# The first context and Wk requested on ScalarE's queue instead of SyncE's, in a gated cross-attention layer

## What is computed

```python
def attention(x, y, Wq, bq, Wk, bk, Wv, bv, Wo, bo):
    q, k, v = split_heads(x @ Wq + bq), split_heads(y @ Wk + bk), split_heads(y @ Wv + bv)
    weights = softmax(q @ k.T / sqrt(32))
    return merge_heads(weights @ v) @ Wo + bo

def quantised_layer(x, weight_q, weight_scale, bias):
    x_scale = maximum(max(abs(x), axis=-1), 1e-6) / 127
    x_q = int8(clip(round(x / x_scale), -128, 127))
    return (x_q @ weight_q.T) * x_scale * weight_scale + bias

x = x + tanh(g_xattn) * attention(layernorm(x), ctx, ...)
x = x + tanh(g_ffn) * quantised_layer(layernorm(x), ...)
```

## Time and profile before

| what | us |
|---|---|
| median of 3 runs | 813.43 (812.89 to 814.37) |
| the profiled execution, its own time | 812.92 |
| its span in the profile | 811.0 |
| TensorE busy | 791.6 |
| VectorE busy | 575.5 |
| ScalarE busy | 555.6 |
| GpSimd busy | 517.4 |

### The profile page before, as it was taken

One profiled execution on the slowest core, in us unless ns is written; L12 is line 12 of the kernel. 1 busy time (PEld: TensorE's weight loads), 2 busy tenths in 40 slices (PEclk: granted clock), 3 DMA queues, 4 the chain that ended last, 5 costly groups with the idle time before them and its releaser, 6 DMA issues.

```text
span 811.0 us, 17119 instructions
## 1 busy us (share of the span) xinstructions
PE 791.6 (98%) x6629; PEld 521.2 (64%) x6658; DVE 575.5 (71%) x916; ACT 555.6 (69%) x845; POOL 517.4 (64%) x518
## 2 busy tenths in 40 slices
PE   8899999999999999999999999999999999999995
PEld 6665667666666666666666666667667666666563
DVE  4878677686767767677586757867678575767668
ACT  5676587676776767676676775767677666777685
POOL 4626484765758566594765758567494765756587
PEclk9999999999999999999999999999999999999998
DMA  8531605142241422315232151422314131111112
GB/s 292 217 83 75 201 28 163 60 144 71 66 132 53 162 79 59 112 53 167 74 117 74 48 172 53 144 79 66 123 54 143 66 92 54 40 53 53 53 52 104
DMA packets 39631, 79.68 MB, mean 98 GB/s; under 512 B 6912, under 2 KB 8320, under 8 KB 37504
## 3 DMA queue, kind: packets, MB, share of 16 engines
q1 hardware_dynamic: 38976, 77.75, 29.8%
q10 hardware_dynamic: 576, 0.85, 0.3%
HBM read 61.78 MB, written 16.81 MB: 97 GB/s over the span
## 4 chain that ended last, share of the span: by engine, by line
PE 89%; DVE 3%; issue 3%; POOL 2%; ACT 1%; DMA 1%; SPq 0%; DVEq 0%; ACTq 0%; POOLq 0%
PE bank_a L340 25%; PE bank_b L340 24%; PE scores L395 8%; PE sum_ps L424 7%; PE scores L412 7%; PE pv_ps L428 6%; PE bank_a L472 3%; PE scores L415 2%; PE pv_ps L472 2%; PE bank_b L472 1%; DVE row_max L1092 1%; PE bank_b L447 1%; PE sum_ps L403 1%; PE bank_a L447 1%; DMA wk_stage<-in_wk 1%
## 5 line engine op out<-in xcount | busy, mean ns | idle before, releaser
L1092 DVE TENSOR_REDUCE row_max<-scores 128x16 f32<-128x1920 f32 x64 | 138.1, 2158 | 109.0 <-PE scores L395 109.0
L773 ACT ACTIVATE probs<-scores 120x2048 f32<-120x2048 f32 x64 | 120.4, 1882 | 77.3 <-PE scores L415 77.2
L1445 POOL TENSOR_TENSOR x<-x,u_sb 128x512 f32<-128x512 f32 x56 | 75.8, 1353 | 127.3 <-DVE u_sb L1181 125.0
L1440 POOL TENSOR_TENSOR x<-x,gbias_r 128x512 f32<-128x512 f32 x64 | 83.0, 1297 | 44.0 <-ACT cen L797 44.0
L395 PEld LDWEIGHTS scores<-k_sb,q_sb 32*128 32x128 f32 x2048 | 63.0, 186 | 53.0 <-issue 41.6
L1432 POOL TENSOR_TENSOR o_lo<-on,o_hi 128x512 fp32r<-128x512 f32 x48 | 62.7, 1307 | 51.7 <-ACT o_hi L791 51.0
L1398 POOL TENSOR_TENSOR xt<-xt,rstd_b 128x512 f32<-128x512 f32 x60 | 92.4, 1564 | 2.3 <-ACT rstd_b L1026 2.3
L1428 POOL TENSOR_TENSOR x<-x,gbo_r 128x512 f32<-128x512 f32 x64 | 88.6, 1396 | 2.4 <-DMA x<-in_x 2.3
L395 PE MATMUL scores<-k_sb,q_sb 32*128 32x120 f32 x2048 | 74.7, 282 | 1.3 <-issue 1.0
L424 PE MATMUL sum_ps<-probs,ones_f 120*32 120x512 f32 x512 | 68.2, 605 | 0.2 <-ACT probs L773 0.2
L428 PE MATMUL pv_ps<-probs,v_sb 120*32 120x512 f32 x512 | 66.6, 592 | 0.0
(11 more groups left out here) (225 smaller groups left out, 2000.4 us busy)
## 6 DMA issues: line engine op xcount, KB each, us to landing
xt<-in_x_t SPq DMA_DIRECT2D x16, 1024.0 KB, 5.6
x<-in_x SPq DMA_DIRECT2D x64, 256.0 KB, 3.0
out_x<-x SPq DMA_DIRECT2D x61, 256.0 KB, 2.1
x_in<-in_x SPq DMA_DIRECT2D x60, 256.0 KB, 3.0
rstd_b<-rstd_rows SPq DMA_DIRECT2D x14, 256.0 KB, 4.7
ctx_sb<-in_ctx_t SPq DMA_DIRECT2D x8, 360.0 KB, 4.8
probs<-in_wq SPq DMA_DIRECT2D x4, 256.0 KB, 3.5
x<-in_wo SPq DMA_DIRECT2D x1, 1024.0 KB, 9.6
```

What stands on the lines that cost most here:

```text
L773: act.activation(probs[0:KEYS], scores[0:KEYS], ACT.Exp, scale=SCALE).then_inc(p_ready, 1)
L1092: dve.tensor_reduce(row_max[:].rearrange("p (t r) j -> p r t j", r=ROWG)[:, :, :, j], scores[:, :, 0:QT * KEYS].rearrange("p r (t k) -> p ...
L1440: pool.tensor_tensor(x1_of(m)[:, t], x1_of(m)[:, t], gbias_r[:], ALU.add).then_inc(x1b_ready, 1)
L1445: pool.tensor_tensor(x1_of(m)[:, t], x1_of(m)[:, t], u_sb[:], ALU.add).then_inc(out_ready, 1)
```

## The change

Three requests leave SyncE's list and stand at the head of ScalarE's, in the same order: the first context (360 KB) and the two halves of Wk (384 KB each). ScalarE's request for the identity (64 KB) comes behind them. The semaphores, the waits, the destinations and everything else stay as they are; later contexts are still requested by SyncE.

```diff
@@ block of SyncE
             for c in range(DT):
                 load(wq_landed[c], wq_stage[:, c], rows(wq)[:, c])
-            load_ctx(0)
-            load(wk_landed[0], wk_stage[:, :, 0:D // 2], rows(wk)[:, :, 0:D // 2])
-            load(wk_landed[1], wk_stage[:, :, D // 2:D], rows(wk)[:, :, D // 2:D])
             load_xt(0)
             for t in range(QT):
                 load(x0_landed[t], x0_stage[t], x_v[0, t])
@@ block of ScalarE
+            def rows(w):
+                return w.rearrange("(c p) n -> p c n", p=P)
...
+            load(ctx_landed, ctx_sb[:], ctx_t[0])
+            load(wk_landed[0], wk_stage[:, :, 0:D // 2], rows(wk)[:, :, 0:D // 2])
+            load(wk_landed[1], wk_stage[:, :, D // 2:D], rows(wk)[:, :, D // 2:D])
             load(ident_landed, ident_stage, consts_f32)
             act.preload_act_table_set("natural_log_exp_and_others")
             act.wait_ge(ident_landed, 16)
```

## The result

| | median us | range us | runs |
|---|---|---|---|
| before, on the same chip | 812.94 | 812.29 to 814.37 | 6 |
| after | 816.86 | 816.12 to 819.75 | 6 |

The ratio is 1.0053, with an interval of 1.0034 to 1.0072: slower by 3.9 us. The forecast was 817.0, in a range of 814.0 to 818.6, slower. So sign and size came out; the steps, as will be seen, did so only in part.

The account below looks back on a forecast made before the run. TensorE, back to back in the steady part, bounds the kernel, so the opening's lateness carries through: the late identity delays the spread by 3.6 us, and 813.43 + 3.6 gives 817.0 us, range 814.0 to 818.6.

Parts of the forecast that it names:

- The order of landings: Opening loads: Wq's last tile at 8.7 instead of 6.8, x transposed 11.7 for 12.4, Wk's second half 13.6, identity 14.3.
- The turns by piece: DMA queues of SyncE and ScalarE alternate by piece, not byte; taken from 74 to 78 packets between 2.5 and 3 us.
- rival B: Queues share by bytes: Wq through at 9.5, K 1.6 us late, identity harmless; 815.0 us, chance 0.12.
- the identity lands with the third x tile: 14.3: ScalarE's queue: the identity, behind the context and Wk, lands at 14.3 instead of 3.82, beside the third x tile.
- the second half of Wk: 13.6: ScalarE's queue: Wk's second half lands with the second x tile at 13.6 instead of 9.9; two K tiles wait.
- Rival D: Faster: earlier requests fill the engines' unused share from 4 to 6 us and win 1.49 us; 812.0 us, chance 0.04.
- ScalarE held up by the identity: ScalarE idle until about 14.3, when the identity lands; its other work follows, with the spread's copy 3.7 us late.
- Its split of Wq moves with ScalarE's: GpSimd's split of Wq shifts 5.95 us with ScalarE's, ending at 20.4 for 14.46; row deviations then end at 22.4.
- the sum of +3.6: TensorE's spread of the row deviations only at 22.4, 3.6 us late; first scores 25.3 for 21.65, carried to the end.
- the mean's 1.17 us: TensorE and VectorE: the mean of Wq ready 1.17 us after Wq's last tile, as before, so at 9.85.
- After that nothing absorbs it, after 40 us nothing waits: TensorE's longest later wait up to 40 us, 0.76, takes nothing off; after 40 us nothing waits for these loads.
- Rival C: Not slower: Wq keeps its place, by 6.8, and GpSimd's 1.95 us wait hides an identity by 10.3; 813.4 us, chance 0.12.

Follow-up runs that it names:

- Experiment 5: Changed kernel with Wk in one request of 2 KB pieces and the identity's request at the head of SyncE's queue: 817.52 us, ratio 1.0054.
- experiment 2: Kernel before with only the identity's request moved, into SyncE's list between the second and third x tile: 818.59 us, ratio 1.0064.
- experiment 3: Changed kernel with ScalarE's wait for the identity and its rounding moved behind the high parts of Wq and x: 814.72 us, ratio 1.0024.
- experiment 1: Changed kernel with the identity's request back at the head of ScalarE's queue: 816.13 us, ratio 1.0038.
- experiment 7: Changed kernel with the identity's rounding behind the splits of Wq and x, and GpSimd's scaling waiting for `max_sp`: 813.92 us, ratio 1.001.
- experiment 6: Changed kernel with one wait added, so GpSimd's third scaling of batch 1 comes after VectorE's `max_sp`: 817.0 us, ratio 1.0044.
- experiment 9: Changed kernel with eight unread products added on TensorE in the gap before the spread: 815.96 us, ratio 1.0039.
- experiment 11: Kernel with Wk in 2 KB pieces and identity first on SyncE, plus four products ahead of each wait for a Wq tile: 816.17 us, ratio 1.0046.
- experiment 10: Changed kernel with eight unread products before the spread and eight more before batch 0's turn of maxima: 816.27 us, ratio 1.0042.

## Why the prediction was right, and where it was not

**The order of landings.** Wq's last tile was forecast for 8.7 and came at 8.59; x transposed was forecast for 11.7 and came at 11.5 (requested at 2.82, 8.7 us to landing). The turns by piece were forecast from one half microsecond and held from 8 to 10 us. Queues of after from 8 to 9 us, and from 4 to 6 (packets, MB, share):

```profile
q1 hardware_dynamic: 52, 0.38, 90.1%
q10 hardware_dynamic: 52, 0.05, 14.9%
...
q10 hardware_dynamic: 381, 0.41, 60.1%
q1 hardware_dynamic: 184, 0.33, 45.1%
```

Equal counts, 0.38 MB against 0.05: rival B, sharing by bytes, is out for this stretch. From 4 to 6 us, however, ScalarE's queue moved two pieces to SyncE's one. These two lines alone would fit shares by bytes (0.41 MB to 0.33). Experiment 5 would not: there both queues' requests were in pieces of 2 KB, and the counts were 276 to 87. So neither rule describes this window. The step "the identity lands with the third x tile: 14.3" failed through this: it came at 12.39, because Wk got ahead early. So did "the second half of Wk: 13.6", which came at 11.5 and made no wait in the K projection. Rival D's premise, an unused share, was true of before from 4 to 6 us (0.76), and in after the share was 1.05. Whether it takes a second queue to fill it is another matter. In experiment 2, where SyncE's queue carried all of it alone, the same window reads:

```profile
4.00:6.00 2.00, 2.00 (x5) 0.98 (x5) 0.00 (x0) 0.00 (x0) 0.00 (x0) 1.00 1.01 308
```

One queue, a share of 1.01, and 308 GB/s. From 2 to 12 us the traces have 344 GB/s in before, 369 in experiment 2 and 374 in after.

The Trainium skill, DMA: Bandwidth & Descriptors (Issuing engines are not separate DMA queues), as drawn on in the prediction, gives a second issuer only the issue time. The two windows from 4 to 6 us show more, 372 for 267 GB/s, but experiment 2 shows that one queue alone can come near it over the opening, so no run here shows a gain from the second queue as such.

**ScalarE held up by the identity.** Right as a mechanism: the split of Wq stands 3.9 us late (12.63 for 8.70) behind it, and experiments 2 and 3 show that this order of two instructions carries about half of the loss (2.1 of 3.9 us by the medians).

**GpSimd.** "Its split of Wq moves with ScalarE's" was right, but I took its length over from before, and it grew from 4.98 to 5.90 us. VectorE's low parts of x, 15.60 to 20.45, now lie beside it, and took 4.85 for 2.46 themselves. In experiments 1, 3, 5 and 7, where the two overlap for 1 us at most, the split took 4.97 to 4.99; in 2, 6 and 9, as in the change, with over 3.5 us of it, 5.89 to 5.91. This gave 0.9 us back to the sum that the early identity had taken out. The deviations ended at 21.33 (forecast 22.4), the spread stood at 21.48, 2.7 us late (forecast 3.6).

The Trainium skill, SBUF — State Buffer (SBUF: two separate sides), has VectorE and GpSimd share a port pair on which, for operations like these with two inputs in SBUF, one shuts the other out for a whole instruction. The trace agrees, with `max_sp` at 1.61 us for 0.25 beside GpSimd's scaling. I had not weighed it, since no engine's own work was changed.

**The clock.** The prediction gave it nothing. I had read before's granted clock as 1.00 all through the opening; the record of it begins only at 4.61 us, and is 1.00 from there. I kept it there although I forecast a new wait on TensorE. In the profiled execution the missing term is 0.83 us, the first scores at 2.00 for 1.17. There the sum of +3.6 meets 3.55 by the last maxima because one term was 0.9 too large and another of 0.8 was missing. That is luck.

It does not account for the median. The executions at 816.12 and 816.40 have a mean granted clock of 0.999. One fall like the first, 3.4 us at half, costs 0.002 of the mean by itself, so they can hardly have had one. (Every trace also has the lower level in its last 1.9 to 4.7 us, so a mean of 0.997 or 0.998 tells nothing.) Experiment 1's profiled execution is a model for them: 816.19 us, 0.999, no fall in its trace, first scores 2.71 late (24.36) and the second `max_sp` 3.2 late (81.58). The median of +3.9 lies between such executions and those that lose more to the clock, 817.32 to 819.75 at 0.995 and 0.992; the one at 816.20 has 0.996 and does not fit this order.

**When the clock first rises.** Before, the chain began with Wk, and TensorE had 1.06 us to spare ahead of the K projection. Now the chain can begin with the mean of Wq, and how fast its products run counts. The traces have the rise at 4.61 in before, 5.69 in after, 8.07 in experiment 9, 9.93 in 3 and 12.23 in 5, and the K projection started at 9.01 (there it waited for Wk), 9.55, 10.02, 10.86 and 12.66. The prediction took the mean's 1.17 us over from before, where the rise had come early. In after's profiled execution that was right.

**"After that nothing absorbs it, after 40 us nothing waits".** The opening's lateness was not absorbed. But `max_sp` met GpSimd's scaling, took 1.36 us longer, and in the profiled execution a second fall of the clock followed. This execution lost 3.3 us more after 38.24 than its lateness there explains (6.84 less 3.54). The same 2.0 us wait stood in the profiled executions of experiments 1 and 2 with the clock at 1.00 from 40 to 50 us, and in those of 3 and 5 with a fall. So the same wait has a fall in some traces and none in others. So does the wait: in experiments 9 and 11 `max_sp` took 0.23 us without an edit there. Experiment 1 has the wait without a fall and loses 0.5 us over this stretch (2.71 at the first scores, 3.20 at the second `max_sp`), so of the 3.3 the larger part goes with the fall. That these falls make the upper end of the six times is argued from the mean granted clocks, 0.992 in the longest and 0.999 in two of the shortest, and is not shown by an edit that removes them alone. A late first rise could do the same and would not show in that mean. Experiments 7 and 10, whose traces have no fall up to 800 us, have narrower spreads, as it would predict.

**Rival C** needed Wq by 6.8 and the identity by 10.3; they came at 8.59 and 12.39. Experiment 7 shows how near it would have been with ScalarE's order mended: ratio 1.001.

**A slip in rival B.** By its own shares the identity is through at 2,384 KB, not 2,448: 168 KB after 9.9, so at 10.3 and not 10.5. It changes no time.

**What stays open:** why ScalarE's queue got two pieces to one from 4 to 6 us, and what makes the clock first rise at 5 us in one execution and at 10 or 12 in another. Of the kernels tried, none beats before.

## What to carry to other kernels

When loads are moved to another engine's queue, look first at what that engine itself waits for and where in its queue this stands: small requests that its first instruction needs belong ahead of bulk, or the instruction behind work that is ready. From 7 to 11 us the two queues shared by piece here, so give each transfer a place by how many pieces it has and how large its neighbours' are; from 4 to 6 us the counts were not equal, so leave some room. And where an edit makes TensorE wait, price the slower clock that can follow, and see which operations of VectorE and GpSimd now fall side by side.

## What the runs showed that I had not expected

- A wait of 2.08 to 2.32 us before the spread came with a granted clock of 0.50 in each profiled execution that had it (after, 2 and 6); one of 2.0 us before the turn of maxima came with a fall in after, 3 and 5 and with none in 1 and 2. The waits of 0.64 to 0.76 had none behind them. The Trainium skill, TensorE: Matmul & The Clock Gate (The HAM clock gate), has the clock go between the same two levels with the engine's activity; the traces agree on the levels.
- A share that one queue left unused from 4 to 6 us in before (0.76) was filled in after (1.05), but in experiment 2 by one queue alone (1.01): one window of one trace does not measure what a queue can do.
- Meeting a neighbour's operation can cost 1.4 us: `max_sp` took 0.25 us in before, and 1.61 in after, where it came just as GpSimd's next operation did.
- A granted clock of 1.00 at the start can mean that nothing is recorded yet: the record began at 4.6 to 12.2 us, and products before it took 1.06 us where those after it took 0.59. So read a row's duration beside the clock.
